# VectorE's and ScalarE's hooks for other stages moved to other steps of a pair of batches, in a fused attention and expert block

## The reference

```python
h = _layernorm(x) * (1 + ca) + sa
x = x + ga * attn(h)     # qkv = h @ W_pack; rope; 2-tap causal conv on k and v; 16 heads, 8 kv heads,
                         # softmax over a window of 128; @ W_o
h = _layernorm(x) * (1 + cb) + sb
x = x + gb * ffn(h)      # rmsnorm; router over 32 experts, top 4, at most 128 tokens per expert;
                         # silu(g) * u @ w_down per expert; plus a shared expert of 704 features
```

## Time and profile before

| what | us |
|---|---|
| three timed runs, median | 818.39 |
| lowest, highest | 815.42, 822.55 |
| the profiled execution | 815.22 |
| its span, first to last instruction | 813.0 |
| first scores of pairs 0, 1, 2, 3 start at | 30.25, 168.93, 307.39, 447.08 |

### The profile page before, as it was taken

The page is one execution under the profiler, slowest core; times in us unless marked ns, Lnnn a source line. Parts: engine busy times, 40 slices in busy tenths (PEclk is TensorE's granted clock), DMA queues, the critical chain, the costliest instruction groups (busy, mean ns, idle before and its releaser), DMA issues.

```text
span 813.0 us, 12301 instructions
## 1 busy us (share of the span) xinstructions
PE 754.8 (93%) x3858; PEld 621.3 (76%) x3858; DVE 544.1 (67%) x1692; ACT 458.0 (56%) x1148; POOL 427.4 (53%) x337
## 2 busy tenths in 40 slices
PE   4878999999999999899999999999889799998997
PEld 2567888887788888778888878888667567776774
DVE  4578776678877768888686786878454115554265
ACT  4667777777787576778676768776352112221110
POOL 0533435554366388645548855655703605675475
PEclk9999999999999999999999999999898989999999
DMA  8943900000004111100401002040368438997671
GB/s 305 306 100 95 341 1 1 2 0 2 1 1 135 48 38 45 38 1 0 155 2 52 36 21 72 2 156 10 107 173 244 123 110 225 296 296 164 151 250 52
DMA packets 62351, 84.45 MB, mean 104 GB/s; under 512 B 6312, under 2 KB 50229, under 8 KB 62288
## 3 DMA queue, kind: packets, MB, share of 16 engines
q1 hardware_dynamic: 53456, 74.04, 29.0%
q0 software_dynamic: 7680, 8.95, 5.5%
q10 hardware_dynamic: 1152, 0.69, 0.3%
HBM read 54.88 MB, written 33.51 MB: 109 GB/s over the span
## 4 chain that ended last, share of the span: by engine, by line
PE 69%; DVE 14%; ACT 8%; issue 5%; another core or an unknown queue 2%; DMA 2%; SPq 0%; POOL 0%; ACTq 0%; DVEq 0%; POOLq 0%
PE PJ L1269 17%; PE OUT L1367 10%; PE U L1356 5%; PE U L1322 5%; PE U L1518 5%; PE U L1345 4%; PE U L1460 3%; PE OUT L1460 3%; PE U L1321 3%; PE U L1357 3%; ACT U L536 2%; PE U L1269 2%; PE XB L1537 2%; PE OUT L1537 2%
## 5 line engine op out<-in xcount | busy, mean ns | idle before, releaser
L731 POOL TENSOR_TENSOR qsw<-qsw,sinT 128x512 f32<-128x512 f32 x96 | 123.7, 1288 | 222.4 <-ACT qsw L523 221.8
L536 ACT ACTIVATE U<-U,nmax 128x128 f32<-128x128 f32 (+1 forms) x256 | 99.1, 387 | 86.7 <-DVE nmax L928 81.5
L928 DVE CUSTOM_DVE_ANT_0 U<-U,mask 128x128 f32<-128x128 f32 (+1 forms) x256 | 86.8, 380 | 74.7 <-PE U L1322 74.4
L1367 PE MATMUL OUT<-wo,oT 128*128 128x256 f32 x512 | 133.3, 384 | 0.0
L1269 PE MATMUL PJ<-hT_hi,w_hi 128*128 128x512 f32 x256 | 112.1, 438 | 0.8 <-issue 0.8
L1269 PE MATMUL PJ<-hT_lo,w_hi 128*128 128x512 f32 x256 | 101.0, 395 | 0.0
L1269 PE MATMUL PJ<-hT_hi,w_lo 128*128 128x512 f32 x256 | 100.9, 394 | 0.0
L735 POOL TENSOR_TENSOR qr<-qr,qsw 128x512 f32<-128x512 f32 x64 | 82.4, 1288 | 30.0 <-DVE qr L916 26.7
L938 DVE TENSOR_SCALAR prob<-U,rinv 128x128 f32<-128x128 f32 (+1 forms) x256 | 95.1, 413 | 4.5
L1367 PEld LDWEIGHTS OUT<-wo,oT 128*128 128x128 f32 x512 | 88.7, 193 | 6.9
L522 ACT ACTIVATE qsw<-PJ 64x512 f32<-64x512 f32 x96 | 57.0, 593 | 63.3 <-PE PJ L1269 57.8
(11 more groups left out here) (202 smaller groups left out, 1596.9 us busy)
## 6 DMA issues: line engine op xcount, KB each, us to landing
wgu<-in_dram SPq DMA_DIRECT2D x32, 352.0 KB
expert_sum<-blank SPq DMA_DIRECT2D x3, 2176.0 KB, 17.3
wd<-in_dram SPq DMA_DIRECT2D x16, 352.0 KB
slot_rows<-blank SPq DMA_DIRECT2D x1, 4624.0 KB, 24.7
xe<-slot_rows SPq DMA_DIRECT2D x16, 289.0 KB, 4.6
late_sums<-expert_sum SPq DMA_DIRECT2D x9, 512.0 KB, 9.8
wraw<-in_dram SPq DMA_DIRECT2D x8, 512.0 KB, 13.3
bcm<-mod_rows SPq DMA_DIRECT2D x8, 512.0 KB, 6.7
```

The costliest lines, as they stand in the source:

```text
L536: last = act.activation(U[n % 3][:, a:z], U[n % 3][:, a:z], ACT.Exp, scale=-1.0, bias=nmax[:, n % 4, j:j + 1], accum_out=rsum[:, n % 4, j: ...
L731: pool.tensor_tensor(pair3(qsw[:, n % NQSW, :]), pair3(qsw[:, n % NQSW, :]), both(sinT[:, :]), ALU.mult).then_inc(t2_done, 1)
L928: last = dve.tensor_tensor_reduce(out=U[n % 3][:, a:z], in0=U[n % 3][:, a:z], in1=mask[:, a:z], scale=-float(HD) ** -0.5, scalar=3.4e38, o ...
L1367: last = pe.matmul(OUT[b][:, t * H:(t + 1) * H], oT[:, n % NOT, t * PN:(t + 1) * PN], wo[:, head, :], start=(head == 0 and t == 0), stop=( ...
```

## The change

No instruction is added or removed. Hooks stand in other steps:

- DVE `prepare_stats`: from steps 0 and 3 of the pair in front to steps 28 and 30 of the pair before that one; for pair 1's rows, which have none before, steps 3 and 5 of pair 0. DVE `prepare_norm`: 8, 9 to 7, 8. `prepare_lo`: 16, 19 to 20, 25.
- DVE `post_stats`: both in step 4, now 4 and 5. `post_h2`: 6, 7 to 9, 11. `post_keys` and `post_carry`: 25 to 26.
- ACT, both square roots: step 5 to 6. `post_squares`: 7, 8 to 10, 12.
- POOL: the first scatter from step 26 to 27; the rule that spreads them is the same, so that the last two now stand in step 7 of the next pair, where one stood.

```diff
--- before.py
+++ after.py
@@ -590,7 +590,7 @@
                 q, _ = next_step(n)
                 if n < 0 or n >= NU:
                     return
-                if l == 5:
+                if l == 6:
                     if q < NPAIR:
                         prepare_norm(q)
                     if p >= 0:
@@ -601,8 +601,8 @@
                     if l in (13, 15):
                         prepare_hi(q, (l - 13) // 2)
                 if p >= 0:
-                    if l in (7, 8):
-                        post_squares(p, l - 7)
+                    if l in (10, 12):
+                        post_squares(p, (l - 10) // 2)
                     if l == 12:
                         post_rms(p)
                     if l in (14, 17):
@@ -761,7 +761,7 @@
                 pool.tensor_tensor(h, h, xres[:, 2 * b:2 * b + 2, :], ALU.add).then_inc(base_done, 1)
 
 
-            FIRST_SCATTER = 26
+            FIRST_SCATTER = 27
             SCATTERS = {}
             at, c = FIRST_SCATTER, 0
             while c < TT * TOPK:
@@ -1083,21 +1083,23 @@
             def hooks(n):
                 p, l = post_step(n)
                 q, _ = next_step(n)
+
+                if q == 1 and l in (3, 5):
+                    prepare_stats(q, (l - 3) // 2)
+                if q + 1 < NPAIR and l in (28, 30):
+                    prepare_stats(q + 1, (l - 28) // 2)
                 if q < NPAIR:
-                    if l in (0, 3):
-                        prepare_stats(q, l // 3)
-                    if l in (8, 9):
-                        prepare_norm(q, l - 8)
-                    if l in (16, 19):
-                        prepare_lo(q, (l - 16) // 3)
+                    if l in (7, 8):
+                        prepare_norm(q, l - 7)
+                    if l in (20, 25):
+                        prepare_lo(q, (l - 20) // 5)
                 if p >= 0:
                     if l in (1, 2):
                         post_gate(p, l - 1)
-                    if l == 4:
-                        post_stats(p, 0)
-                        post_stats(p, 1)
-                    if l in (6, 7):
-                        post_h2(p, l - 6)
+                    if l in (4, 5):
+                        post_stats(p, l - 4)
+                    if l in (9, 11):
+                        post_h2(p, (l - 9) // 2)
                     if l in (13, 14):
                         post_xn(p, l - 13)
                     if l in (15, 18):
@@ -1110,7 +1112,7 @@
                         post_slots(p)
                     if l == 24:
                         post_probs(p)
-                    if l == 25:
+                    if l == 26:
                         post_keys(p)
                         post_carry(p)
                 if p == LAST - 1 and l in (16, 19, 20, 28):
```

## The result

| | before | after |
|---|---|---|
| median of twelve runs each, us | 818.89 | 822.48 |
| lowest, highest | 815.02, 823.24 | 818.73, 824.09 |
| the profiled execution, and its span | 815.22, 813.0 | 821.53, 819.4 |
| first scores of pairs 0, 1, 2, 3 start at | 30.25, 168.93, 307.39, 447.08 | 30.02, 170.67, 309.24, 450.12 |

The ratio of after to before is 1.0046, with a 95% interval of 1.0025 to 1.0067: about 3.8 us slower, where 0.8 us slower was forecast. That is within the 1% that I called no change, and inside the range.

A forecast was written before the change was run, and what follows sets the result against it. PE was taken as the bound (busy 754.8 of 813.0 us), so only its waits could be won. Pair 0 +1.55, pairs 1 and 2 -0.7 each, pair 3 +0.6 gave about +0.8: 819.2 us, range 811 to 828.5.

The forecast's parts named there:

- wrong if: Sign of failure: step 14 stays at 4.7 us, or the granted clock falls behind its wait.
- Steps 7 to 10: Pairs 1 and 2: the 4.05 us lost here falls to 0.4; pair 1 takes near 17 us instead of 20.5.
- table loads: ACT's two loads, moved from step 5 to 6: 0.4 us late at step 8 in each of pairs 1 to 3.
- wins nothing by itself: Next rows' statistics leaving steps 0 and 3 in pairs 1 to 3: no gain, since they cost PE nothing there.
- Steps 13 and 14: Pairs 1 to 3: second squares and second h2 lengthen ACT's chain of step 12; 3.3 us lost where 0.39 stood.
- the bound of 4.6: Upper bound on the 3.3 us lost in steps 13 and 14, if h2 is blocked by a POOL multiply.
- rival C: Moved VectorE operations meet POOL's multiplies more often, 1.0 us a meeting: 823 us profiled, 826 as a median; chance 0.10.
- The squares: Second squares, put ahead of ACT's chain in step 12, which has no slack: 0.9 us in full.
- Rival B: Step 14's wait lowers PE's granted clock in three pairs: 5.2 us or twice that, 824 to 830 median; chance 0.18.
- Pair 0: Statistics +0.95 us, table loads +1.2 (0 to 2.6), xin wait gone -0.6: sum +1.55, bounds -0.5 and +3.
- Rival A: Faster, the late place does not fill again: -8.1 us, 805 to 807 profiled, 808 to 810 median; chance 0.13.
- lo, keys and post_stats: Moved DVE hooks, each batch about 0.7 to 1.0 us, within DVE's 1.07 us free per step: counted as 0.

The follow-up runs named there:

- the combined version: Changed kernel with h2 in steps 9, 10, squares in 10, 11, second post_xn in 16, pair 0's statistics and roots back: 808.27 us, ratio 0.9896.
- post_xn alone: Kernel before with post_xn of the second batch in step 16 instead of 14, nothing else: 812.59 us, ratio 0.9954.
- Pair 0 as before: Changed kernel with pair 0's statistics back in steps 0 and 3 and its square roots in step 5, norm still moved: 819.45 us, ratio 1.0020.

## Why the prediction was right or wrong

**Time.** 819.2 was forecast, 822.5 measured: no change, as forecast, but the 0.8 us that I added up lies outside the interval of the measured difference (2.0 to 5.5 us). By its own signs the prediction failed in one: it is "wrong if" the granted clock falls behind the wait in step 14, and it fell there in pairs 1 and 2. In the profile, the 127 steps took 5.5 us longer after, 3.1 when both kernels were profiled again; the ratio, 3.8 us, lies between. Pair by pair, profiled again: +2.86, +0.06, -0.40 and +0.55 us, where +1.55, -0.7, -0.7 and +0.6 were forecast. The low clock in steps 21 and 22 is in no term of the sum and in no rival; it added 3.2 us in one profile of the changed kernel and nothing in the other.

**Steps 7 to 10: right.** "Pair 1's steps 7 to 10 near 17 us": 16.77. Of the 4.05 us lost there, 0.32 is left, in step 8, for the table loads, put at 0.4; the combined version with the roots in step 5 had the same 0.4 there. That the statistics' leaving steps 0 and 3 "wins nothing by itself" may be too low: without it 0.61 and 1.08 us stayed in step 7 of pairs 1 and 2. The first h2 cost nothing, and the norm's wait went.

**Steps 13 and 14: right.** The forecast was 3.3 us where 0.39 stood. In pair 3, where the clock stays up, step 13 loses 0.59 and step 14 7.15 - 4.32 = 2.83: 3.42 us. The chain that I named is the one that bounds it. Two of its terms hid errors that cancel. Moving the second h2 by one step took 7.15 - 5.52 + 0.59 = 2.2 us off these steps in pair 3, about the 2.0 that I had put on it, but its own duration was 3.0, with one L987 blocked by POOL: I had kept that as the bound of 4.6 (my terms give 3.3 + 1.0 = 4.3) and under rival C. The squares, put at 0.9 "in full", gave 0.8 in pair 3 and 0.2 in pairs 1 and 2 when taken away from step 12, since ACT's step 11 is full there, too.

**Rival B came true in two of three pairs, at its price.** I gave it 0.18 and 1.7 us for each fall, "from a wait of about 2.5 us on"; the waits were 2.55 us, the price 1.68, and the stretch's clock 0.63. The forecast left it out, and that is its first error. What I held against B, a wait of 3.65 us with no fall behind it, was the exception of one profile: behind the same wait (3.64 to 3.66 us) the clock fell in the other thirteen. And 2.5 us was no bound: a wait of 2.09 us at 81.86 in the run with post_xn alone has a fall behind it, those of 2.54 to 2.56 us in pair 3 of four profiles have none. What B lacked was the repayment: steps 15 and 16 give 1.04 back, so the net is 0.64 us each, 1.3 together, and not 5.2 or more. Without it pair 1 changes by 138.57 - 138.46 - 0.64 = -0.5 us and pair 2, profiled again, by 139.35 - 139.75 - 0.64 = -1.0, against the forecast of -0.7 each; I had taken pair 2 like pair 1, but its step 7 took 6.43 us before, not 5.96. Pair 3, profiled again, changed by 133.24 - 132.69 = +0.55, against +0.6.

**Pair 0: the second error, and the larger one.** Forecast +0.95 + 1.2 - 0.6 = +1.55. Measured between profiles with like starts: +0.95 for the statistics, +2.6 for the loads and -0.7 for xin, together +2.85 (the pair took 2.86 us more when both were profiled again). The statistics' 0.95 "in full" was right. The step that failed is "of which I take 1.2 us as new waits (0 to 2.6)": ACT's loads in step 6 stand behind the weight half, with nothing free before the next head, so that 2.6 of their 2.9 us came through, my upper bound. Pair 0 as before took (1.0046 - 1.0020) x 818 = 2.1 us off the median, with intervals of 1.7 and 2.7 us to either side, and 3.6 us off pair 0 in the traces.

**Rival A** (step 14 doesn't fill again) fell. But more than half of its -8.1 us is what h2 in step 10 shows: 0.9941, 4.8 us below before. "ACT cannot use time in which it waits for DVE's scores" was right only as long as an h2 stood in front of those scores in step 11.

**Rival C** took part in the h2 of step 11, once in each pair as before in step 7, not in its other places: the first h2 is unblocked (0.99 and 0.88 us), and both L896 take 0.73 and 0.84 as forecast.

**lo, keys and post_stats**: no step shows them; counted at 0, right. The scatters' 0 is within what was measured (1.0012, 0.9969 to 1.0055), and no sharper than that.

**What remains open**: whether the first scatter's step has a part in the last wait; how h2's lateness divides into its own length and the blocked 1.0 us; how far the moved hooks bring about the low clock in steps 21 and 22; and why the same wait of 2.55 us lowered the clock in pair 3 of one kernel and not of the other.

## What to carry to other kernels

In a loop where TensorE is full and two other engines have about 1 us free in each step, as here, spreading hooks evenly isn't enough: a hook that is longer than the free time of its step (here 2.0 us against 1.07) needs an empty step behind it on its own engine and on the one that it makes late, and none of them may be the step of the other engine's longest chain (here ACT's two table loads). List, for each step, what is free on both engines, place the fixed chain first, and then the long hooks as far ahead of it as their data allow. Where a wait of over 2 us appears on TensorE, look at the granted clock behind it and at the next wait, which may pay part of it back. And take a second profile of both kernels before a difference of some us is put down to the change.

## What the runs showed of the hardware that I hadn't expected

The granted clock fell without any wait of PE. In step 21 PE runs 24 router matmuls of 34 columns, 0.11 us apart, from 404.06 to 406.74, and then the usual ones of 512 columns. The end of the one and the start of the other in PE's timeline after:

```profile
406.63 0.26 PE L1271 MATMUL XB<-wr_hi,xnT_lo 128*128 128x34 f32 x1
406.74 0.48 PE L1271 MATMUL PJ<-hT_hi,w_hi 128*128 128x512 f32 x1
407.06 0.59 PE L1271 MATMUL PJ<-hT_lo,w_hi 128*128 128x512 f32 x1
```

The row at 407.06 takes 0.59 us, where this form takes 0.39 elsewhere; the window from 407 to 411, above, has 0.57 with PE busy for all of it. It stands in one to three pairs of eight of the ten profiles with h2 moved, in no pair of the four without (before, twice; scatters alone; post_xn alone), and costs 1.6 us each time. What decides it isn't known. In the combined version the clock falls there in pairs 2 and 3 (7.29 + 4.81 us for steps 21 and 22, where 10.48 is usual), so some 3 us would be won, by this estimate, if it stayed up.
